# Post-norm transformer layer in fp32 on one core: Silu table and rounding of y moved, two output tiles moved into the last attention group, x transposes and one weight transpose rescheduled

## The reference

```python
def attn(x, w_qkv, b_qkv, w_out, b_out):
    qkv = x @ w_qkv.T + b_qkv                 # split into q, k, v of 16 heads
    scores = q @ k.T / sqrt(32) + causal      # -inf above the diagonal
    out = softmax(scores) @ v
    return out @ w_out.T + b_out

def ffn(x, ...):
    Wg, Wu, Wd = (w - 128.0) * scale[:, None] # for gate, up and down
    return (silu(x @ Wg.T) * (x @ Wu.T)) @ Wd.T

x = layernorm(x + attn(x, ...))
x = layernorm(x + ffn(x, ...))
```

## Time and profile before

| | us |
|---|---|
| Median of 3 runs (lowest, highest) | 780.61 (779.65, 783.03) |
| The profiled execution | 784.28 |
| Its span | 782.1 |
| TensorE busy | 744.8 |
| VectorE, ScalarE, GpSimd busy | 395.1, 387.4, 128.2 |
| TensorE's share of the chain that ended last | 90% |
| Mean granted clock of TensorE, share of full | 0.98 |

### The profile page before, as it was taken

The page is one execution under the profiler, slowest core; times in us unless marked ns, Lnnn a source line. Parts: engine busy times, 40 slices in busy tenths (PEclk is TensorE's granted clock), DMA queues, the critical chain, the costliest instruction groups (busy, mean ns, idle before and its releaser), DMA issues.

```text
span 782.1 us, 11953 instructions
## 1 busy us (share of the span) xinstructions
PE 744.8 (95%) x4480; PEld 571.0 (73%) x4480; DVE 395.1 (51%) x1006; ACT 387.4 (50%) x914; POOL 128.2 (16%) x148
## 2 busy tenths in 40 slices
PE   7998899999999999999899999899999999999993
PEld 6776576776767677776578887688887888788882
DVE  4755666567566666567542222353326432463236
ACT  3754766666766666676555655422224222322220
POOL 0000110315131050301834123200000000000001
PEclk9999899999999999999899999999999999999997
DMA  9201413335521364302568954511210010000201
GB/s 316 89 0 28 135 59 77 81 83 122 151 79 55 88 183 136 73 12 73 124 148 184 224 176 139 178 63 40 68 55 0 13 58 36 0 1 27 81 1 55
DMA packets 59719, 68.67 MB, mean 88 GB/s; under 512 B 33552, under 2 KB 35600, under 8 KB 59536
## 3 DMA queue, kind: packets, MB, share of 16 engines
q1 hardware_dynamic: 53456, 49.05, 21.0%
q0 software_dynamic: 6208, 18.88, 10.2%
HBM read 59.53 MB, written 14.68 MB: 95 GB/s over the span
## 4 chain that ended last, share of the span: by engine, by line
PE 90%; DVE 4%; ACT 3%; issue 1%; DMA 1%; POOLq 0%; SPq 0%; POOL 0%; DVEq 0%; ACTq 0%
PE bank L1365 15%; PE bank L1366 15%; PE bank L1158 12%; PE bank L1234 9%; PE bank L1371 7%; PE bank L1372 7%; PE bank L1173 6%; PE bank L1217 5%; PE bank L1255 5%; PE bank L1192 5%; ACT probs L710 1%; DVE probs L917 1%; PE bank L1266 1%; PE bank L1130 1%; PE bank L1120 1%
## 5 line engine op out<-in xcount | busy, mean ns | idle before, releaser
L710 ACT ACTIVATE probs<-probs,neg_max 128x128 f32<-128x128 f32 (+3 forms) x256 | 140.4, 552 | 12.7 <-DVE neg_max L917 12.7
L1033 DVE SCALAR_TENSOR_TENSOR hid<-bank,u_scale,silu 128x512 f32<-128x512 f32 x64 | 48.1, 751 | 176.2 <-PE bank L1366 174.1
L917 DVE CUSTOM_DVE_ANT_0 probs<-bank,causal 128x128 f32<-128x128 f32 (+3 forms) x256 | 111.6, 484 | 29.1 <-PE bank L1217 27.8
L1365 PE MATMUL bank<-xT_hi,gateT 128*128 128x512 f32 x256 | 101.9, 398 | 5.7 <-DVE xT_lo L1042 3.8
L823 ACT ACTIVATE hid_hi<-hid 128x512 fp32r<-128x512 f32 x64 | 40.5, 632 | 122.5 <-DVE hid L1033 122.5
L1366 PE MATMUL bank<-xT_lo,gateT 128*128 128x512 f32 x256 | 101.1, 395 | 0.0
L1371 PE MATMUL bank<-downT,hid_hi 128*128 128x512 f32 x256 | 99.9, 390 | 0.9 <-DVE hid_lo L1036 0.8
L1365 PE MATMUL bank<-xT_hi,upT 128*128 128x512 f32 x256 | 100.3, 392 | 0.0
L1366 PE MATMUL bank<-xT_lo,upT 128*128 128x512 f32 x256 | 100.1, 391 | 0.0
L1372 PE MATMUL bank<-downT,hid_lo 128*128 128x512 f32 x256 | 99.7, 389 | 0.0
L1234 PEld LDWEIGHTS bank<-ident,probs 128*128 128x128 f32 x640 | 75.0, 144 | 30.5 <-issue 15.8
(11 more groups left out here) (94 smaller groups left out, 1137.5 us busy)
## 6 DMA issues: line engine op xcount, KB each, us to landing
scan_buf<-in_L_ffn_gate_w_dram SPq DMA_DIRECT2D x4, 1024.0 KB, 5.1
scan_buf<-in_L_ffn_up_w_dram SPq DMA_DIRECT2D x4, 1024.0 KB, 5.2
scan_buf<-in_L_ffn_down_w_dram SPq DMA_DIRECT2D x4, 1024.0 KB, 5.2
y_scratch<-z_tok SPq DMA_DIRECT2D x16, 256.0 KB, 5.0
x_tok<-y_scratch SPq DMA_DIRECT2D x4, 1024.0 KB, 6.1
w_int<-in_L_ffn_gate_w_dram POOLq DMA_DIRECT2D x16, 256.0 KB, 3.1
w_int<-in_L_ffn_up_w_dram POOLq DMA_DIRECT2D x16, 256.0 KB, 2.9
w_int<-in_L_ffn_down_w_dram POOLq DMA_DIRECT2D x16, 256.0 KB, 3.8
```

Source lines behind the costliest of these rows:

```text
L710: nc.scalar.activation(probs[qb][:, j, :], probs[qb][:, j, :], ACT.Exp, bias=neg_max[:, qb, j:j + 1], scale=-1.0, accum_out=row_sum[:, qb, ...
L917: nc.vector.tensor_tensor_reduce(out=probs[qb][:, j, :], in0=score[j][:, first:first + w], in1=causal[:, S - w:S], scale=-SCALE, scalar=-F ...
L1033: nc.vector.scalar_tensor_tensor(out=hid[:, i % 2, :], in0=bank[:, :], scalar=u_scale[:, i:i + 1], in1=silu[:, i % 2, :], op0=ALU.mult, op ...
L1365: nc.tensor.matmul(acc[n][:, :], w[:, c, cols], form(xT_hi[:, c, :]), start=c == 0, stop=False)
```

## The change

Five edits:

- `W_STEPS`: weight tile 15 goes from (2, 2) to (2, 13). `SCAN_AT` stays.
- In group 2 the four transposes of x go to steps 1, 2, 4, 5 (`X_FIRST`); those of groups 6, 10 and 14 stay.
- Output tiles 0 and 1 of batch 3 get banks 0 and 1 (score banks), and nine products each are issued at step 5 of group 15, after the maxima of query block 3 of head 0 and 1.
- An ACTIVATE with Silu on 128 x 1 stands ahead of the last `att_hi`; of the down pieces of chunk 0 two go ahead of the loop and two behind silu 0; tile 0's gate and up use banks 2 and 3, so that tile 1's need not wait for hidden 0 (they wait for output tiles 0 and 1 to be drained).
- `y_hi(0, c)` for c = 0, 1, 2 goes into iteration 15 of batch 0, ahead of the last piece, c = 3 behind it, all inside the conditional block.

```diff
--- before.py
+++ after.py
@@ -65,12 +65,13 @@
     INVERSE_STEP = 15
     SLOTS = 6
     X_STEPS = [4, 4, 6, 6]
+    X_FIRST = [1, 2, 4, 5]
 
 
     W_TILES = [(kind, n) for n in range(2) for kind in "qk"] + [("v", t) for t in range(NT)] + [
         (kind, n) for n in range(2, NG) for kind in "qk"] + [("o", n) for n in range(ND)]
     NW = len(W_TILES)
-    W_STEPS = {(0, 4): 8, (0, 7): 9, (1, 2): 12, (1, 4): 10, (1, 7): 11, (1, 9): 13, (1, 13): 14, (2, 2): 15}
+    W_STEPS = {(0, 4): 8, (0, 7): 9, (1, 2): 12, (1, 4): 10, (1, 7): 11, (1, 9): 13, (1, 13): 14, (2, 13): 15}
 
 
     W_ORDER = list(range(8)) + [W_STEPS[at] for at in sorted(W_STEPS)]
@@ -87,6 +88,14 @@
     MM = 3 * ND
     LAST = B - 1
     EVEN = [8, 0, 0, 4, 0, 4, 8, 0, 6, 0, 6, 0, 6, 0, 0, 6]
+
+    def of_steps(jobs, skip):
+        counts = list(EVEN)
+        for s in range(STEPS):
+            taken = min(skip, counts[s])
+            counts[s], skip = counts[s] - taken, skip - taken
+            counts[s] = max(0, min(counts[s], MM * len(jobs) - sum(counts[:s])))
+        return jobs, counts
 
     def filling(G):
         b, g = divmod(G, NG)
@@ -102,13 +111,7 @@
         if g == 3:
             return ([("v", b + 1, 0), ("v", b + 1, 1)] + ahead, EVEN) if b < LAST else ([], [0] * STEPS)
         before = [("o", b - 1, t) for t in range(QH, NT)] if b > 0 else []
-        jobs = before + ahead
-        counts, skip = list(EVEN), 2 * MM - len(before) * MM
-        for s in range(STEPS):
-            taken = min(skip, counts[s])
-            counts[s], skip = counts[s] - taken, skip - taken
-            counts[s] = max(0, min(counts[s], MM * len(jobs) - sum(counts[:s])))
-        return jobs, counts
+        return of_steps(before + ahead, 2 * MM - len(before) * MM)
 
     def tasks_at(s):
         return [i for i in range(BLOCKS) if TASK_STEPS[i] == s]
@@ -117,7 +120,7 @@
         return [m for m in range(len(PRODUCTS)) if PRODUCT_STEPS[m] == s]
 
     def x_at(G, s):
-        return [t for t in range(NT) if X_STEPS[t] == s] if G % NG == 2 else []
+        return [t for t in range(NT) if (X_STEPS if G > NG else X_FIRST)[t] == s] if G % NG == 2 else []
 
     FILLING = [filling(G) for G in range(GROUPS)]
 
@@ -132,6 +135,8 @@
 
     WORK = 3
     PLACE = {}
+
+    OUT_STEP = 5
 
     class Banks:
 
@@ -175,11 +180,12 @@
             if s == INVERSE_STEP:
                 banks.whole(("r", G))
             banks.part(jobs, sum(counts[:s]), counts[s])
-    for t in range(NT - 1):
+    for t in range(QH):
+        PLACE["o", B - 1, t] = (WORK + t, 0)
+    for t in range(QH, NT):
         banks.start(("o", B - 1, t))
-    for t in range(NT - 1):
+    for t in range(QH, NT):
         banks.end(("o", B - 1, t))
-    banks.whole(("o", B - 1, NT - 1))
 
     y1_dram = nc.dram_tensor("y1_scratch", (B * S, D), F32, kind="Internal").ap()
 
@@ -199,12 +205,12 @@
 
 
 
-    FIRST_PIECES = [("g", 0), ("u", 0), ("g", 1), ("u", 1)] + [("d", 0, t) for t in range(ND)]
+    FIRST_PIECES = [("g", 0), ("u", 0), ("g", 1), ("u", 1), ("d", 0, 0), ("d", 0, 1)]
 
     def pieces_at(i):
 
         r, t = i // TPR + 1, i % TPR
-        return ([("g", i + 2), ("u", i + 2)] if i + 2 < NI else []) + [("d", r, t) if r < NI // TPR else ("y", t)]
+        return ([("d", 0, 2), ("d", 0, 3)] if i == 0 else []) + ([("g", i + 2), ("u", i + 2)] if i + 2 < NI else []) + [("d", r, t) if r < NI // TPR else ("y", t)]
 
     PIECES = FIRST_PIECES + [p for i in range(NI) for p in pieces_at(i)]
     WEIGHTS = [p for p in PIECES if p[0] != "y"]
@@ -325,7 +331,7 @@
         exact_weights, wide_weights = (gateT, upT, downT), (gateT_wide, upT_wide, downT_wide)
 
         bank = [ctx.enter_context(nc.psum_tensor(f"bank{i}", [P, 512], F32)) for i in range(8)]
-        score, work, pv_acc = bank[0:HG], bank[HG:HG + WORK], bank[HG + WORK]
+        score, work, pv_acc = bank[0:HG], bank[HG:HG + WORK] + bank[0:QH], bank[HG + WORK]
         gate_acc, up_acc, down_acc = bank[0:4:2], bank[1:4:2], bank[4:8]
         piece_bank = [gate_acc[1], up_acc[1]]
 
@@ -341,8 +347,8 @@
         x_loaded = sem("x_loaded")
         z_loaded = sem("z_loaded")
         res_ready = sem("res_ready")
-        work_full = [sem(f"work_full{i}") for i in range(WORK)]
-        work_drained = [sem(f"work_drained{i}") for i in range(WORK)]
+        work_full = [sem(f"work_full{i}") for i in range(WORK + QH)]
+        work_drained = [sem(f"work_drained{i}") for i in range(WORK + QH)]
         x_hi_done = sem("x_hi_done")
         score_full = [sem(f"score_full{j}") for j in range(HG)]
         max_done = sem("max_done")
@@ -415,6 +421,10 @@
                 return downT[:, TPR * n:TPR * (n + 1), piece[2] * P:(piece[2] + 1) * P]
             return yT_next[:, n, :].rearrange("p (t q) -> p t q", t=NT)
 
+        def first_bank(i):
+
+            return 1 if i == 0 else 0
+
         def full_by(n, weights):
 
             return n + 1 if weights is wide_weights else sum(piece[0] == "y" for piece in PIECES[:n + 1])
@@ -768,6 +778,7 @@
                         w_hi(W_STEPS[G, s])
                     if (G, s) in SCAN_AT:
                         scan(SCAN_AT.index((G, s)))
+            nc.scalar.activation(minus_exact[:, :], half_power[:, 0:1], ACT.Silu).then_inc(act_warm, 1)
             att_hi(GROUPS - 1)
 
 
@@ -822,12 +833,12 @@
 
                 nc.scalar.activation(hid_hi[:, i % HIDS, :], hid[:, i % 2, :], ACT.Copy).then_inc(hid_hi_done, 1)
 
-            def y_hi(b):
-
-                act.wait_ge(up_full, (b + 1) * NI)
-                for c in range(ND):
-                    act.wait_ge(yT_kept, b * ND + c + 1)
-                    nc.scalar.activation(xT_hi[:, c, :], yT_next[:, c, :], ACT.Copy).then_inc(yT_hi_done, 1)
+            def y_hi(b, c):
+
+                if c == 0:
+                    act.wait_ge(up_full, (b + 1) * NI)
+                act.wait_ge(yT_kept, b * ND + c + 1)
+                nc.scalar.activation(xT_hi[:, c, :], yT_next[:, c, :], ACT.Copy).then_inc(yT_hi_done, 1)
 
             def first_batch(weights):
                 for n in range(len(FIRST_PIECES)):
@@ -842,11 +853,18 @@
                 act.wait_ge(scales_loaded, 48)
                 n = len(FIRST_PIECES)
                 for i in range(NI):
-                    gate_out(0, i, gate_acc[0])
+                    gate_out(0, i, gate_acc[first_bank(i)])
+                    early = 2 if i == 0 else 0
+                    for m in range(early):
+                        evict_piece(n + m, weights)
                     hidden_hi(0, i)
-                    for m in range(len(pieces_at(i))):
+                    if i == NI - 1:
+                        for c in range(ND - 1):
+                            y_hi(0, c)
+                    for m in range(early, len(pieces_at(i))):
                         evict_piece(n + m, weights)
                     n += len(pieces_at(i))
+                y_hi(0, ND - 1)
 
             act.wait_ge(scan_done, 1)
             wide = act.value_load(wide_flag[0:1, 0:1], min_val=0, max_val=1)
@@ -855,7 +873,6 @@
             with act.If(wide > 0):
                 shift_piece(0)
                 first_batch(wide_weights)
-            y_hi(0)
 
             def ffn_batch(b, ahead):
                 turns = turns_of(ahead)
@@ -870,7 +887,8 @@
                         gate_out(b, i, gate_acc[n % 2])
                         hidden_hi(b, i)
                 if ahead:
-                    y_hi(b)
+                    for c in range(ND):
+                        y_hi(b, c)
 
             with act.Fori(1, B - 1) as b:
                 ffn_batch(b, True)
@@ -1068,7 +1086,7 @@
             variance(B - 1, mv_done, var_done)
             dve.wait_ge(scales_loaded, 48)
             for i in range(NI):
-                hidden(0, i, up_acc[0])
+                hidden(0, i, up_acc[first_bank(i)])
             y_lo(0)
             for t in range(NT):
                 drain_down(0, t)
@@ -1286,6 +1304,8 @@
                 transpose_weights(2 * n + 4)
                 transpose_weights(2 * n + 5)
 
+            outs = [project_out(B - 1, t) for t in range(NT)]
+
             for G in range(GROUPS):
                 b, g = divmod(G, NG)
                 jobs, counts = FILLING[G]
@@ -1295,6 +1315,11 @@
                         ahead, qbs = SCORE_STEPS[s]
                         if G + ahead < GROUPS:
                             scores(G + ahead, qbs)
+                    if G == GROUPS - 1 and s == OUT_STEP:
+                        for t in range(QH):
+                            pe.wait_ge(max_done, (G * NT + NT - 1) * HG + t + 1)
+                            for _ in range(MM - 3):
+                                next(outs[t])
                     for i in tasks_at(s):
                         transpose_task(G, i)
                     for t in x_at(G, s):
@@ -1314,8 +1339,7 @@
             for m in products_at(STEPS):
                 weighted_values(GROUPS - 1, m)
 
-            outs = [project_out(B - 1, t) for t in range(NT)]
```

(15 more changed lines are left out.)

## The result

The changed kernel takes 788.19 us (median of 5 runs, 787.01 to 789.37), the kernel before in the same session 780.91 us (779.65 to 783.03): a ratio of 1.0087, 95% interval 1.0066 to 1.0108. It is slower by 0.9%; the forecast was slower by 0.6% (785.0 us, range 780 to 790). The changed kernel's profiled execution took 789.37 us.

The account below looks back on a forecast made before the run. TensorE bounds the kernel, computing 744.8 of 782.1 us, so only its gaps and half-rate stretches count. Terms +12.8 - 1.3 - 1.4 - 5.7 = +4.4 us on the median 780.61 gave 785.0 us, range 780 to 790.

Parts of the forecast that it names:

- Part 2: Tile 15 to step 13, group 2: late scan load delays inverse sums 10.2 us, low clock 2.6; +12.8 us (11.5 to 14).
- Part 1: Group 2's x transposes at steps 1, 2, 4, 5: first product of q earlier; 1.3 us won (0.5 to 2.9).
- Parts 3 and 4: Group 15 and feed-forward start: DMA transposes hold silu 1, gate 2 starts at 411.5 us; 1.4 us won (0.5 to 3.9).
- Part 5: y roundings moved into the last iteration: gap between feed-forward batches 0 and 1 and half clock behind it go; 5.7 us won.
- rival C: Between feed-forward batches: TensorE pays 2.6 us for entering the loop, half clock stays; part 5 gives 1.4, 789.3 us; chance 0.14.
- Rival A: Group 2: scan load is no limit, so part 2 costs nil; 772.2 us, faster; chance 0.08.
- rival B: Feed-forward start: DMA transposes don't hold silu 1, 8.2 us won instead of 1.4; 778.2 us; chance 0.12, other larger gains included.
- I put the difference on the median: Final step: the +4.4 us, reckoned from the 784.28 us profiled execution, put on the 780.61 us median; 785.0 us.

Follow-up runs that it names:

- experiment 1: Changed kernel with weight tile 15 back at step 2 of group 2, nothing else undone: 777.62 us, ratio 0.9955 to the kernel before.
- Experiment 2: Kernel before with weight tile 15 moved to step 13 of group 2 as the one edit: 790.87 us, ratio 1.0128.
- experiment 4: Changed kernel with weight tile 15 at step 10 instead of 13: 781.69 us, ratio 1.0003 to the kernel before.
- experiment 9: Changed kernel with tile 15 at step 2, down pieces one iteration later, group 2's x transposes again at steps 4, 4, 6, 6: 768.62 us.
- experiment 3: Changed kernel with down pieces of chunks 1 to 3 widened one iteration later, tile 15 still at step 13: 781.82 us, ratio 1.0007.
- experiment 6: Changed kernel with tile 15 at step 2 and the 18 output products put behind group 15 again: 775.75 us, ratio 0.9926.
- experiment 7: Changed kernel with tile 15 at step 2, the 18 output products behind group 15 again, down pieces one iteration later: 773.86 us, ratio 0.9911.
- experiment 11: The kernel before, unchanged, profiled a second time: profiled execution 783.40 us, span 781.2.
- experiment 8: Changed kernel with tile 15 at step 2, down pieces one iteration later, all y roundings behind the conditional block again: 774.23 us, ratio 0.9900.
- 12: Changed kernel with tile 15 at step 7 and down pieces one iteration later: 767.84 us, ratio 0.9818 to the kernel before.

## Why the prediction was right

The direction and its main reason were right; the size was 4.4 us forecast against 7.3 us.

**Part 2** (tile 15 to step 13): the chain is shown by experiments 1, 2 and 4, and every step of it stands in the profile. Its size was too large. Experiment 2, the tile alone, measures +9.3 us by the medians and +9.5 in the stretch from the inverse sums of group 1 to those of group 3 (57.6 against 48.1), not 12.8, and its low end (11.5) was too high as well. The step at fault is "Its four transposes only move": taken away from step 2, the tile no longer holds VectorE's maxima back (2.2 us), and its own transposes no longer stand ahead (0.5). TensorE reaches the tile's new place at 93.95 us where 98.49 was forecast, 3.6 us sooner when counted from the inverse sums of group 1 (72.20 and 73.17). From there on the forecast was near: 11.3 us to the inverse sums of group 2 (forecast 10.6), and 2.2 for the low clock behind (2.6).

**Part 1** (spread of x): forecast 1.3 us won. The two starts that it rests on were hit in the changed kernel (task 4 at 86.53 us, forecast 86.6; the first product of q at 89.01, forecast 89), but with the tile gone and no spread the first product of q starts earlier still, at 86.72 (experiment 2). Beside that kernel the spread costs 0.6 to 2.0 us in that stretch (58.2 and 59.7 against 57.6), since the low halves of x now stand ahead of the maxima; with the tile at step 2 it is worth nothing (experiment 9). By the medians the tile costs 10.6 us with the spread (experiment 1) and 9.3 without, which fits, but no run has this difference clear of the noise. That parts 1 and 2 together come to +11.3 us in the table where +11.5 was forecast is by these figures luck: 3.3 us too much loss in the one, and 1.9 to 3.3 too little in the other.

**Parts 3 and 4**: that silu 1 would wait for SP behind the down piece is shown by experiment 3, and the forecast start of gate 2 (411.5 plus 11.5) was hit within 0.4 us. That the lower clock would take back most of it was right too, but the gain was taken too large and the clock too small: the start of gate 2 came 3.3 us earlier relative to group 3 (3.9 forecast), and the stretch from 423.3 to 430 at 0.53 cost 3.1 (2.5 forecast). So 0.3 us was left of the forecast 1.4, outside its ends (0.5 to 3.9). Experiments 6 and 7 show what the forecast only implied: the 18 products are worth nothing while the down piece holds, 3.6 us once it doesn't.

**Part 5** (y): forecast 5.7, in the profile 5.8 (+11.0 at down 15, +5.2 at gate 1 of batch 1). TensorE pays nothing visible for entering the loop: rival C is refuted by the timeline at 507.6 us. The undoing costs 2.7 us by ratios and 4.0 by medians, without the table load.

**Rival A** fell with experiment 2, **rival B** with the last issue at 418.6 and experiment 3.

**What was off in the sum.** Its own range, "781.5 to 788.5 by the ends of parts 1, 2 and 4", doesn't follow from these ends, which give 779.6 to 787.9. And its last step, "I put the difference on the median", carried gains read from one profile over to medians. All gains together were 8.4 us by the forecast and 7.4 us by the profiles (782.1 against 774.7), but 3.9 us by the medians of experiment 1. Part 2 was oversized by 3.5 us, the gains by 4.5, and the two errors partly cancel. The profile of the kernel before shows it at a mean granted clock of 0.980, where its other executions have 0.984 in the median (experiment 11), so it had more half-rate work to win back than they have on average; that is some 1.4 of the 3.5 us between 7.4 and 3.9, and the rest is open. The medians of experiments 1 and 2 add up to +5.4 us against the 7.3 measured; the cost of the spread with a late tile, 0.6 to 2.0, is of that size.

## What to carry to other kernels

When a step is moved in a hand-written order, look for every queue that waits for it, not only for who reads its result, and for what its leaving frees at the old place: here a transpose moved by eleven steps held a DMA load in SP's queue, which held a scan in ScalarE's, which held a bank. A gap that is filled is worth its length only if the next limit isn't already as near; where it is, the filled work comes back as a longer gap with its own stretch of low clock. Take a second profile, and weigh a difference of spans by how far each profiled execution stands from its own median, in time and in mean granted clock.

## What the runs showed of the hardware that was not expected

ScalarE stands idle for 2.6 us where it leaves the conditional block, with a table load behind it (2.60 us, before) and without any (2.62, experiment 8), while TensorE, entering its loop from within its own block, shows 0.23 us from product to product. The time of an execution goes with its mean granted clock: 50 executions of one kernel lie between 0.980 and 0.990 and between 778.05 and 784.18 us. One version (12) keeps the full clock from 10 us to the tail, although TensorE still waits in group 2, 1.4 and 1.2 us at the longest.
